# Last feed-forward of a four-layer cross-attention stack: its inner normalisation moved behind the second product, with rows made ahead

## The reference

```python
def _L3_ffn_ref(x, W_fc, ln_w, ln_b, W_proj):      # LN_EPS = 1e-05
    # absmean(W) = sign(W/g) * min(round(|W/g|), 1), g = mean(|W|) + 1e-6: entries -1, 0, 1
    h = jnp.einsum('btd,hd->bth', x, absmean(W_fc))          # 128 -> 512
    h = jax.nn.gelu(h, approximate=False)
    h = layernorm(h, ln_w, ln_b)                             # over the 512, then * ln_w + ln_b
    return jnp.einsum('bth,dh->btd', h, absmean(W_proj))     # 512 -> 128
...
x = x + _L3_xattn_ref(_layernorm(x, axis=-1), ctx_768, ...)
x = x + _L3_ffn_ref(_layernorm(x, axis=-1), ...)
return x
```

## Time and profile before

| | us |
|---|---|
| median of 3 runs | 554.53 |
| the profiled execution | 553.32 |
| its span | 551.4 |
| PE busy | 482.9 (88%) |
| DVE busy | 382.7 (69%) |
| ACT busy | 268.8 (49%) |
| POOL busy | 155.4 (28%) |

### The profile page before, as it was taken

The page is one execution under the profiler, slowest core; times in us unless marked ns, Lnnn a source line. Parts: engine busy times, 40 slices in busy tenths (PEclk is TensorE's granted clock), DMA queues, the critical chain, the costliest instruction groups (busy, mean ns, idle before and its releaser), DMA issues. The chain is left out here.

```text
span 551.4 us, 9333 instructions
## 1 busy us (share of the span) xinstructions
PE 482.9 (88%) x3139; PEld 335.9 (61%) x3139; DVE 382.7 (69%) x1365; ACT 268.8 (49%) x819; POOL 155.4 (28%) x185
## 2 busy tenths in 40 slices
PE   3960699999988999988889899989999999889977
PEld 2420689898544566776546456757666666557945
DVE  3799988935775566853787678855445556789776
ACT  2698387520524666633256346641222221778643
POOL 4999993030233600001302631111000000020042
PEclk9665579999999999998899999999999999999999
DMA  7104000000373000000011400000000000000001
GB/s 267 60 1 153 1 2 3 1 1 14 141 303 135 1 2 1 2 2 1 0 36 36 116 0 1 2 1 2 1 1 0 1 0 2 0 2 0 2 0 39
DMA packets 8453, 18.37 MB, mean 33 GB/s; under 512 B 1171, under 2 KB 6611, under 8 KB 7894
## 3 DMA queue, kind: packets, MB, share of 16 engines
q1 hardware_dynamic: 8406, 17.78, 9.1%
HBM read 15.99 MB, written 1.79 MB: 32 GB/s over the span
## 5 line engine op out<-in xcount | busy, mean ns | idle before, releaser
L212 POOL TENSOR_SCALAR rtmp<-mv 128x4 f32<-128x4 f32 x18 | 4.4, 245 | 239.4 <-DVE mv L191 208.9
L1878 PEld LDWEIGHTS bank<-arenaA,arenaB 128*128 128x128 f32 x320 | 38.7, 192 | 8.4 <-issue 7.2
L1889 ACT ACTIVATE xt<-bank 128x512 f32<-128x512 f32 x26 | 15.6, 598 | 54.3 <-PE bank L1862 53.2
L1940 DVE TENSOR_TENSOR arenaB<-xt,bank 128x512 f32<-128x512 f32 x26 | 17.9, 687 | 34.5 <-PE bank L1863 31.8
L1862 PE MATMUL bank<-xnT,arenaA 128*128 128x512 f32 x80 | 41.1, 595 | 0.7 <-ACT xnT L270 0.7
L1863 PE MATMUL bank<-xnT,arenaA 128*128 128x512 f32 x80 | 40.9, 592 | 0.0
L263 PE MATMUL bank<-in_ctx 128*128 128x512 f32 (+2 forms) x112 | 39.7, 490 | 0.0
L1878 PE MATMUL bank<-arenaA,arenaB 128*128 128x128 f32 x320 | 38.8, 275 | 0.0
L1100 DVE TENSOR_REDUCE nmax<-bank 128x1 f32<-128x512 f32 x32 | 20.5, 684 | 13.2 <-PE bank L1043 13.2
L263 PEld LDWEIGHTS bank<-in_ctx 128*128 128x128 f32 x112 | 18.9, 203 | 14.5 <-issue 13.9
L1863 PEld LDWEIGHTS bank<-xnT,arenaA 128*128 128x128 f32 x80 | 15.2, 190 | 19.1 <-issue 19.1
(11 more groups left out here) (486 smaller groups left out, 1283.6 us busy)
## 6 DMA issues: line engine op xcount, KB each, us to landing
arenaA<-in_moe_dram SPq DMA_DIRECT2D x1, 3840.0 KB, 11.6
in_dft<-in_dft_dram SPq DMA_DIRECT2D x1, 2048.0 KB, 7.4
in_dft<-in_head_dram SPq DMA_DIRECT2D x1, 2048.0 KB, 7.5
arenaA<-in_l_dram SPq DMA_DIRECT2D x1, 2048.0 KB, 16.1
vw_scratch<-in_dft SPq DMA_DIRECT2D x32, 38.5 KB
arenaB<-vw_scratch SPq DMA_DIRECT2D x2, 576.0 KB, 4.8
in_rows<-in_rows_dram SPq DMA_DIRECT2D x1, 842.5 KB, 7.0
in_ctx<-in_ctx_dram SPq DMA_DIRECT2D x1, 653.0 KB, 6.0
```

Of the source, the lines that this page charges most:

```text
L1878: ins = nc.tensor.matmul(bank[4 + m % 2][:, q4 * P:(q4 + 1) * P], hid2[:, m % 2, c, q4 * P:(q4 + 1) * P], w[:, 2 * HE + c * P:2 * HE + (c ...
L1889: nc.scalar.activation(sil2[n % 3], bank[n % 2][:], ACT.Silu).then_inc(silu_ready, 1)
L1940: Vv.tensor_tensor(hid2[:, m % 2, c, :], sil2[n % 3], bank[2 + n % 2][:], ALU.mult).then_inc(hid_ready, 1)
```

## The change

Mathematically, with m and r the mean and reciprocal root of a tile's GELU output g, the second product of (g - m) r w + b is

r (g w) Wp + r (-m) (w Wp) + b Wp

The changed kernel sends g itself through the transposes and multiplies it by w only. The two rows w Wp and b Wp are made ahead by PE, into the free half of bank 5, in tile 0 of the last attention (`pe_rows4`), each broadcast over all partitions, and copied to SBUF by two DVE instructions (L2204, L2205; the first is negated). After the second product DVE forms a = (-row) m + product (L2379) and then X = a r + X (L2383), with a wait for itself between. POOL adds the row b Wp into X for four tiles at a time (`pool_rows4`, L2345 of the changed kernel).

The first up product (`pe_up4(pe, 0)`) moves into the output product of the last attention tile, between its fourth and fifth accumulated part. A GELU of one column is put ahead of ACT's copy of the turned first half, so that the table load stands there. PE turns the second half at n == 2 of its loop instead of n == TB, and DVE normalises it at n == 0 instead of n == 1. The transposes of a tile are one step of the loop earlier, at t = n - 1.

```diff
@@ pe_attend3
+                        if t == 0 and g == 2:
+                            pe_rows4(pe)
                         for c in range(4 * g, min(4 * g + 4, CK3)):
...
                     for c in range(CK3):
                         w = min(P, HK3 - c * P)
+                        if t == NT - 1 and c == 4:
+                            pe_up4(pe, 0)
                         ins = nc.tensor.matmul(bank[6 + t % 2][:, 0:P], pT3[0:w, t % 2, c, :], vw3[0:w, t // TB, c, :],
@@ vec_attend3
+                    if t == 0:
+                        dve.wait_ge(wsum_mm, 2)
+                        Vv.tensor_scalar(rows4[:, 0, :], bank[5][:, 2 * P:3 * P], -1.0, None, ALU.mult)
+                        Vv.tensor_copy(rows4[:, 1, :], bank[5][:, 3 * P:4 * P]).then_inc(w3_act, 1)
                     Vv.tensor_copy(pT3[:, t % 2, 8, :], bank[5][:, 0:P])
@@
+        def pe_rows4(pe):
+            pe.wait_ge(tern_ready, 1)
+            for i, name in enumerate(("ln3w", "ln3b")):
+                for c in range(4):
+                    ins = nc.tensor.matmul(bank[5][:, (2 + i) * P:(3 + i) * P], V[name][:, c:c + 1].broadcast_to([P, P]),
+                                           V["wpT"][:, c * P:(c + 1) * P], start=(c == 0), stop=(c == 3))
+            ins.then_inc(wsum_mm, 1)
+        def pe_up4(pe, n):
+            pe.wait_ge(ln_T, NB * 8 + n // TB + 1)
+            if n >= 2:
+                pe.wait_ge(g3_ready, n - 1)
+            nc.tensor.matmul(bank[2 + n % 2][:], xnT[:, n * P:(n + 1) * P], V["wfcT"], start=True, stop=True).then_inc(h3_mm, 1)
@@ pe_l3f
-            pe.wait_ge(tern_ready, 1)
-            for n in range(NT + 4):
-                if n < NT:
-                    if n == TB:
-                        pe_turn(pe, ln_done, NT * 10, xn, [1])
...
-                t = n - 2
+            for n in range(NT + 2):
+                if 0 < n < NT:
+                    pe_up4(pe, n)
+                t = n - 1
                 if 0 <= t < NT:
-                    pe.wait_ge(g3_norm, t + 1)
+                    pe.wait_ge(g3_ready, t + 1)
+                    if t == 1:
+                        pe.wait_ge(x3_added, NT)
...
-                        ins = nc.tensor.transpose(..., g3n[:, t % 3, c * P:(c + 1) * P], ident)
+                        ins = nc.tensor.transpose(..., g3[:, t % 3, c * P:(c + 1) * P], ident)
-                t = n - 3
+                t = n - 2
                 if 0 <= t < NT:
                     pe.wait_ge(g3T_dve, t + 1)
                     pe.wait_ge(g3T_act, t + 1)
+                    if t == 1:
+                        pe.wait_ge(ln_T, NB * 8 + 2)
                     if t >= 2:
-                        pe.wait_ge(x4_added, t - 1)
+                        pe.wait_ge(a4_ready, t - 1)
...
+                if n == 2:
+                    pe_turn(pe, ln_done, NT * 10, xn, [1])
@@ act_l3f
+            nc.scalar.activation(g3[:, 0, 0:1], V["half"][:, 0:1], ACT.Gelu)
+            act_turned(act, 8, which=[0])
...
                     if n >= 3:
-                        act.wait_ge(g3_norm, n - 2)
+                        act.wait_ge(mv3_ready, n - 2)
+                        act.wait_ge(g3_turned, n - 2)
...
-                        ins = nc.scalar.activation(..., ACT.Identity, scale=V["ln3w"][:, c:c + 1], bias=V["ln3b"][:, c:c + 1])
+                        ins = nc.scalar.activation(..., ACT.Copy, scale=V["ln3w"][:, c:c + 1])
@@ pool_l3f
+        def pool_rows4(pool, b):
+            pool.wait_ge(w3_act, 4)
+            pool.wait_ge(ln_done, NT * 10 + TB * (b + 1))
+            r = halves()[b]
+            nc.gpsimd.tensor_tensor(X[:, r], X[:, r], bm(rows4[:, 1, :], TB), ALU.add).then_inc(tern_ready, 1)
...
+                if t == 0:
+                    pool_rows4(pool, 0)
+                if t == 2:
+                    pool_rows4(pool, 1)
@@ vec_l3f
+                if n == 0:
+                    vec_normalise(dve, 10, X, xn, [1])
                 t = n - 1
-                    Vv.tensor_scalar(g3n[:, t % 3, :], g3[:, t % 3, :], mv3[:, t, 0:1], rd3[:, t:t + 1], ALU.subtract, ALU.mult).then_inc(g3_norm, 1)
-                if n == 1:
-                    vec_normalise(dve, 10, X, xn, [1])
-                t = n - 2
...
-                                               V["ln3w"][:, c:c + 1], V["ln3b"][:, c:c + 1], ALU.mult, ALU.add)
+                                               V["ln3w"][:, c:c + 1], None, ALU.mult)
...
                 t = n - 3
                 if 0 <= t < NT:
+                    dve.wait_ge(mv3_ready, t + 1)
                     dve.wait_ge(y4_mm, t + 1)
-                    Vv.tensor_tensor(X[:, t, :], bank[t % 2][:, 0:P], X[:, t, :], ALU.add).then_inc(x4_added, 1)
+                    Vv.scalar_tensor_tensor(a4[:, t % 2, :], rows4[:, 0, :], mv3[:, t, 0:1], bank[t % 2][:, 0:P], ALU.mult, ALU.add).then_inc(a4_ready, 1)
+                    dve.wait_ge(a4_ready, t + 1)
+                    dve.wait_ge(rd3_ready, t + 1)
+                    dve.wait_ge(tern_ready, 2 + t // TB)
+                    Vv.scalar_tensor_tensor(X[:, t, :], a4[:, t % 2, :], rd3[:, t:t + 1], X[:, t, :], ALU.mult, ALU.add).then_inc(x4_added, 1)
```

More of the change, by code:

```diff
@@ L2220, in program @@
         g3 = part(arenaB, 0, 3, HID3)
-        g3n = part(arenaB, 1536, 3, HID3)
+        a4 = part(arenaB, 1536, 2, P)
+        rows4 = part(tmp2[:].rearrange("p t d -> p (t d)"), 0, 2, P)
         g3T = part(arenaB, 3072, 3, HID3)
@@ L2279, in pe_l3f @@
                     for c in range(4):
-                        ins = nc.tensor.transpose(bank[4 + 2 * (t % 2) + c // 2][:, (c % 2) * P:(c % 2 + 1) * P], g3n[:, t % 3, c * P:(c + 1) * P], ident)
+                        ins = nc.tensor.transpose(bank[4 + 2 * (t % 2) + c // 2][:, (c % 2) * P:(c % 2 + 1) * P], g3[:, t % 3, c * P:(c + 1) * P], ident)
                     ins.then_inc(g3_turned, 1)
-                t = n - 3
+                t = n - 2
                 if 0 <= t < NT:
@@ L2307, in act_l3f @@
                     for c in range(2):
-                        ins = nc.scalar.activation(g3T[:, t % 3, c * P:(c + 1) * P], bank[4 + 2 * (t % 2)][:, c * P:(c + 1) * P], ACT.Identity,
-                                                   scale=V["ln3w"][:, c:c + 1], bias=V["ln3b"][:, c:c + 1])
+                        ins = nc.scalar.activation(g3T[:, t % 3, c * P:(c + 1) * P], bank[4 + 2 * (t % 2)][:, c * P:(c + 1) * P], ACT.Copy,
+                                                   scale=V["ln3w"][:, c:c + 1])
                     ins.then_inc(g3T_act, 1)
+                if n == 2:
+                    act_turned(act, 8, which=[1])
+        def pool_rows4(pool, b):
[3 more added lines that the diff above has]
+            nc.gpsimd.tensor_tensor(X[:, r], X[:, r], bm(rows4[:, 1, :], TB), ALU.add).then_inc(tern_ready, 1)
         def pool_l3f(pool, st):
```

20 lines of the change are left out of this document (5 added, 15 removed).

## The result

The changed kernel takes 556.57 us (median of 11 runs, 554.64 to 557.45) against 554.24 us for the kernel before, run beside it (11 runs, 552.98 to 555.2): a ratio of 1.0045, interval 1.0034 to 1.0056. It is 2.3 us slower by the medians, 2.5 by the ratio (1.9 to 3.1). The forecast was 553.6, with 0.08 for slower. The profiled execution took 555.67 us with a span of 553.7, which is 0.9 us under its median, as the profiled execution of the kernel before (553.32) is under the 554.24.

A forecast was written before the change was run, and what follows sets the result against it. Bound: VectorE's chain in the last attention, the stall before the first down product, then PE and VectorE equally at 2.19 us per tile. Last stage -1.36 plus copies +0.40 gave -0.96 us: 553.6, range 552.9 to 554.8.

The forecast's parts named there:

- Step 1: Last attention, tile 0: row products hidden in PE's 1.81 us idle time; two DVE copies move everything behind 0.40 us later.
- Step 2: Attention to last feed-forward: first up product at 522.54 inside last attention product; second half's rstd 0.86 later; table load neutral.
- rival D: ACT table load ahead of the turned half's copy: a drain keeps ACT closed, total 554.2 us; chance 0.04.
- step 3: Last feed-forward: first down product at 530.02, 1.02 us earlier, after PE idles 2.6 us waiting for DVE.
- step 4: Last feed-forward's steady state: PE at 2.19 us per tile without a hole, DVE at 1.99; fifth up product at 533.64.
- Point 6: Last feed-forward, other queues: POOL's two 128x512 row adds cost nothing unless they hold up an rstd.
- Rival C: PE's clock falls in the new 2.6 us hole before the first down product: +2.3 us, 556.9; chance 0.08.
- steps 4 and 5: Last feed-forward to end: PE bound at 2.19 us per tile, then DVE-bound drain; last add at 546.71, 1.36 earlier.
- Gamma pair: DVE's two gamma instructions per tile in the last feed-forward: 0.34 and 0.26, 0.60 us for the pair.
- rival A: Last feed-forward's gamma pass keeps its two-operand price (0.40 and 0.32): gain only 0.27 us, 554.25; chance 0.13.

The follow-up runs named there:

- e5: Kernel before plus only the row products and their two copies in attention tile 0, rows unread: 554.9 us, ratio 1.0037.
- e11: Changed kernel with copies in attention tile 1, row add moved, gamma passes first, and first up product back behind the last attention product: 550.91 us, ratio 0.9945.
- e12: Changed kernel with copies in attention tile 1, row add moved, gamma passes first, and no early one-column GELU: 550.33 us, ratio 0.9937.
- e1: Changed kernel with GpSimd's first row add behind the rstd of tile 1 instead of tile 0: 554.33 us, ratio 1.0003.
- e6: Changed kernel with GpSimd's 128x512 row add cut into four 128x128 adds at the same place: 555.14 us, ratio 1.0038.
- e10: Changed kernel with only the row copies moved from attention tile 0 to tile 1: 555.75 us, ratio 1.0026.
- e14: Changed kernel with copies in attention tile 1, row add behind the rstd of tile 1, two fillers before the first down product: 553.26 us, ratio 0.9986.
- e15: Changed kernel with copies in attention tile 1 and two filler products before the first down product, row add unmoved: 553.86 us, ratio 0.9988.
- e3: Changed kernel with the first row add behind the rstd of tile 1 and three filler products before the first down product: 554.25 us, ratio 0.9989.

## Why the prediction was wrong

**Step 1, rows made ahead: the size right, its consequence missed.** The products went into PE's hole (480.43, 1.95 us, and the scores at 482.62, 0.38 later as everything else), and the copies moved the front by 0.38 where 0.40 was forecast. What failed is the next sentence, that everything behind merely moves: the 0.4 us lengthened a hole of PE's on which the clock hung. e5 shows the price of the step, 1.3 to 2.0 us. With the copies in tile 1 the hole is as before and the clock stayed in seven profiles of seven.

**Step 2, first up product and table: right, and worth nothing.** up(0) came at 523.31, 0.77 later than forecast as was the turn before it. The GELU followed the load after 0.02 us, so rival D was wrong. The Trainium skill (ScalarE: Activation LUTs, "What ACT_TABLE_LOAD costs") states a drain of about 1380 ns with every switch; this trace does not show it. By e11 and e12 neither edit carries a gain that can be told; the forecast priced up(0) only inside step 3 and never against PE's own order, in which up(1) covers the first GELU.

**Steps 3 and 4, from PE's hole to up(4): these are the steps that failed.** Step 3 left PE idle for 2.6 us before y(0), and step 4 ran PE at full clock behind it, from y(0) at 530.02 to up(4) at 533.64, or 3.62 us. The fall of the clock was a term put at nothing. Measured were 5.01 us in the changed kernel and 5.29 to 5.30 in e1, e6 and e10, against 3.63 where fillers stood in the hole (e14): 1.4 to 1.7 us lost, the largest single term and enough by itself to turn the gain of 1.0 into a loss.

**Point 6, the adds on POOL: it missed the meeting.** It said that they "cost nothing unless they hold up an rstd", and step 3 took the normalisation at 1.03 from the earlier trace rows. They hold up VectorE. In the profiled execution that was 1.04 us (9.87 against 8.83 us from the turn to y(0); the forecast was 530.02 - 521.21 = 8.81, and e1, e10, e14 have it). The meeting went one way in one profile and the other way in three, and its mean share was not measured. The Trainium skill (SBUF — State Buffer, "Who interferes with whom") has the mechanism, for VectorE instructions that use both of their ports, as it says that `tensor_scalar` can: whichever of the two engines issues first has the shared ports for its whole instruction, and the other waits. e6 agrees, and both orders occur here. I had weighed the adds by their queue alone.

**Rival C: the right mechanism, the wrong chance.** It was given 0.08 on the ground that the stretch would be about as full as one that kept 1.00. Fullness over nine us hid what was new: the work before had holes of at most 1.4 us there, the new order has one of 2.5. Nor was the fall at 258 us the only one far ahead, as the forecast had it: the hole of 1.62 us at 272 us, with its fall from 274 to 279, was in the same trace. The clock fell in all four profiles with such a hole (changed, e1, e6, e10), and in none of the five in which fillers stood in it. The price was 1.4 to 1.7 us, not 3.3, because the clock was low for 3.4 us and not for 6.6; that its 556.9 lies near the result is luck, since the attention's fall was not in it.

**The rest of steps 4 and 5: nearly right.** Gamma pair 0.57 to 0.59 (0.60; rival A wrong), a and X 0.38 apart. Without the losses (e14) the last stage is 25.85 where 25.50 was forecast: y(0) to up(7) 10.38 instead of 10.19, because every other y is one of 1.13 us, and the drain 6.64 instead of 6.50. So the gain is 1.01 us, not 1.36.

**The sum.** By the profiles: -1.0 for the new order (e14), +0.4 for the copies, +1.6 for the slow clock in the last stage (27.45 - 25.85, e10 and e15), 1.7 x 5/9 = +0.9 for the slow clock in the attention, 1.04 x 1/4 = +0.3 for the meeting: +2.2, against 2.3 measured (2.4 with e3's long fall at its 3.0 us). The two shares are counts of nine and four profiles, so their terms are rough, and the agreement is partly luck. The same terms fit e6 (2.1, measured 2.1), e15 (-0.7, measured -0.7) and, within its interval, e10 (0.9, measured 1.4), but not e1: they give +1.9 there, and measured were +0.2 (-1.2 to +1.6). If that is not chance, either the meeting goes against VectorE more often than in one profile of four, or the clock falls in the attention less often than in five of nine. The profiled executions do not settle it: that of the changed kernel, without the fall in the attention, is 0.9 us under its median, but so is that of the kernel before, whose hole of 1.56 us no profile shows with a fall. So the three causes are shown, each by an edit that takes it away, and how the 2.3 us divide between them is open.

Why the clock falls behind 1.95 us in some executions and not in others, and behind 1.62 us elsewhere in nearly all, stays open.

## What to carry to other kernels

Before an edit that moves work off a path, list the holes of the matrix engine that it makes or lengthens, one by one and not only as a busy share over a stretch, and price a fall of the clock behind each hole longer than any that the trace shows to be harmless at that place. Look through the whole trace for falls and what stood before them: a length that is harmless in one place was not in another. Put small preparatory work where its engine waits anyway: the same two copies cost 1.3 to 2.0 us in one tile of the attention (e5), and in the next nothing that its profiles show. When an add goes to GpSimd, look at what VectorE runs at that moment, also where nobody waits for the add.

## What the runs showed of the hardware

- At the two places of the change the granted clock fell from 2.4 to 1.2 GHz behind holes of PE of 2.5 us and more every time (4 of 4), behind 1.95 us in 5 of 9 profiles, behind 1.56 us in 0 of 8. At a third place, at 272 us, it fell behind 1.62 us in 16 of 17. It stayed low for some 3.4 us, or 6.8. Two fillers of 128x512 (1.88 us of otherwise useless work) in the hole of 2.5 us kept it up and paid 1.6 us (e10 and e15).
- A GpSimd add of 128x512 made a VectorE normalisation of 341 ns take 1390, and cut in four, 585. The other way round, the add took 1.42 us instead of 1.26.
